# New tables of jobs, PSUM banks, engine order, adapter loads and diagonals in a fused adapter, state-space and mixture kernel

## Time and profile before

| | us |
|---|---|
| median of three runs (lowest, highest) | 960.28 (951.68, 961.02) |
| the profiled execution | 949.75 |
| its span, first to last instruction | 948.0 |
| PE (TensorE matmul) busy | 846.9 (89%) |
| DVE (VectorE) busy | 758.0 (80%) |
| POOL (GpSimd) busy | 659.5 (70%) |
| ACT (ScalarE) busy | 631.2 (67%) |

### The profile page before, as it was taken

How to read it: one execution, slowest core, us unless ns; L and a number is a source line. 1 busy time by engine, 2 the same in 40 slices (tenths; PEclk the granted TensorE clock), 3 DMA queues, 4 the chain that set the end, 5 groups by cost and what they waited for, 6 DMA issues and landing times.

```text
span 948.0 us, 18370 instructions
## 1 busy us (share of the span) xinstructions
PE 846.9 (89%) x6328; PEld 758.9 (80%) x6328; DVE 758.0 (80%) x677; ACT 631.2 (67%) x1467; POOL 659.5 (70%) x343
## 2 busy tenths in 40 slices
PE   5695898889997999889997999889997999788976
PEld 4573897789977998789987998789887998587773
DVE  3215776988989889988988889888988888999892
ACT  3227575867767776768767776668766776778650
POOL 1002676678877888668876887768877788889790
PEclk9897799999999999999999999999999999989896
DMA  9994687367662777376663777276773764243211
GB/s 252 316 310 137 222 251 211 107 198 243 171 213 87 274 205 217 109 237 213 170 218 105 255 205 235 78 250 201 194 212 113 223 170 148 90 145 84 90 62 44
DMA packets 165832, 172.23 MB, mean 182 GB/s; under 512 B 85225, under 2 KB 138473, under 8 KB 157550
## 3 DMA queue, kind: packets, MB, share of 16 engines
q1 hardware_dynamic: 143854, 94.12, 35.7%
q10 hardware_dynamic: 21888, 76.95, 23.5%
HBM read 137.33 MB, written 33.69 MB: 180 GB/s over the span
## 4 chain that ended last, share of the span: by engine, by line
PE 64%; DVE 15%; SPq 5%; POOL 5%; issue 4%; ACT 4%; DMA 2%; POOLq 0%; DVEq 0%; ACTq 0%
PE jb L956 28%; PE yp L1124 16%; DVE h L925 10%; PE dBx L956 9%; POOL hC L517 5%; PE yp L956 4%; PE jb L960 3%; PE yp L960 2%; SPq L316 2%; ACT dA L554 2%; SPq L391 2%; DVE Bd L757 1%; DVE dt L742 1%; PE yp L1129 1%; DVE xT L837 1%
## 5 line engine op out<-in xcount | busy, mean ns | idle before, releaser
L517 POOL TENSOR_TENSOR hC<-h,Cb 128x1024 f32<-128x1024 f32 x256 | 612.4, 2397 | 186.0 <-DVE h L925 178.2
L925 DVE TENSOR_TENSOR_SCAN h<-dA,dBx 128x1024 f32<-128x1024 f32 x256 | 583.1, 2281 | 62.6 <-PE dBx L956 51.1
L554 ACT ACTIVATE dA<-dt,negA 128x252 f32<-128x252 f32 x1024 | 430.2, 494 | 81.2 <-DVE h L925 69.8
L1124 PE MATMUL yp<-ident,hC 128*128 128x128 f32 x2048 | 279.7, 282 | 7.7 <-DVE HL L833 3.1
L956 PE MATMUL jb<-xT,Wst 128*128 128x256 f32 x1536 | 239.7, 300 | 17.3 <-DVE dt L742 8.5
L1124 PEld LDWEIGHTS yp<-ident,hC 128*128 128x128 f32 x2048 | 241.9, 146 | 10.7 <-POOL hC L517 7.9
L956 PEld LDWEIGHTS jb<-xT,Wst 128*128 128x128 f32 x1536 | 203.4, 196 | 22.9 <-DVE dt L742 9.9
L956 PE MATMUL dBx<-Bd,stacked 96*128 96x256 f32 x1024 | 189.8, 309 | 19.3 <-DVE h L925 10.0
L956 PEld LDWEIGHTS dBx<-Bd,stacked 96*128 96x128 f32 x1024 | 147.9, 198 | 44.2 <-issue 41.4
L502 POOL TENSOR_TENSOR dtx<-dt,u 128x256 f32<-128x256 f32 x64 | 47.4, 740 | 78.7 <-DVE dt L742 72.6
L579 ACT ACTIVATE HL<-yp 128x256 fp32r<-128x256 f32 x62 | 23.4, 377 | 42.1 <-PE yp L960 39.8
(11 more groups left out here) (145 smaller groups left out, 681.9 us busy)
## 6 DMA issues: line engine op xcount, KB each, us to landing
Wst<-W_scratch ACTq DMA_DIRECT2D x54, 1024.0 KB, 5.8
stacked<-dtx_scratch SPq DMA_DIRECT2D x192, 128.0 KB, 2.7
dtx_scratch<-HL SPq DMA_DIRECT2D x64, 256.0 KB, 2.5
Cb<-c_scratch SPq DMA_DIRECT2D x32, 512.0 KB, 5.5
W_scratch<-Wst ACTq DMA_DIRECT2D x8, 1024.0 KB, 6.1
xres<-in_x SPq DMA_DIRECT2D x64, 128.0 KB, 3.9
out<-obuf SPq DMA_DIRECT2D x32, 256.0 KB, 2.5
xin<-in_x ACTq DMA_DIRECT2D x28, 256.0 KB, 6.5
```

The source lines that it names most:

```text
L517: pool.tensor_tensor(hC[:, un % NHC, :].rearrange("p (n b t) -> p b n t", n=HS, b=2), h[:, un % NH, :].rearrange("p (b n t) -> p b n t", n ...
L554: act.activation(dA[:, half % NDA, :].rearrange("p (b n t) -> p b n t", b=GB_, n=HS)[:, :, n, 1:STEPS], dt[:, j % NDT, :].rearrange("p (b ...
L925: dve.tensor_tensor_scan(h[:, un % NH, :], dA[:, half % NDA, UNIT * p:UNIT * (p + 1)], dBx[un % 2][:, :], 0.0, ALU.mult, ALU.add).then_inc ...
L1124: last = pe.matmul(y, hC[:, un % NHC, P * n:P * (n + 1)], ident[:, :], is_transpose=True, start=un == 0 and n == 0, stop=False, skip_group ...
```

## The change

Only tables change: in which unit each job stands and in which order within one, the chunks of cond in each unit, some banks (xT 0 and 2, stack 7), which evacuations are late on ScalarE and VectorE, the units of `DTX`, `DU`, `ADAPTERS` and `DIAGONALS`, and a table of its own for group 0 in place of one derived from JOBS. The functions that read the tables stay, and so do the operations.

```diff
--- before.py
+++ after.py
@@ -38,50 +38,74 @@
 
 
 JOBS = {
-    (0, 0): [job("A2T", 0, "Y"), job("cond", 1, "A", (3, 5))],
-    (0, 1): [job("cond", 1, "A", (5, 8))],
-    (0, 2): [job("stack", 2, "Y"), job("x1T", 0, "B"), job("cond", 2, "A", (0, 6)), job("x1T", 1, "B")],
-    (0, 3): [job("cond", 2, "A", (6, 7)), job("x1T", 2, "B")],
-    (1, 0): [job("cond", 2, "A", (7, 8))],
-    (1, 1): [job("cond", 3, "A", (0, 3)), job("stack", 3, "Y"), job("x1T", 3, "B")],
-    (1, 2): [job("dtz", 2, "B"), job("cond", 3, "A", (3, 7))],
+    (0, 0): [job("cond", 1, "A", (1, 6))],
+    (0, 1): [job("cond", 1, "A", (6, 8)), job("A2T", 0, "Y")],
+    (0, 2): [job("stack", 2, "Y"), job("x1T", 0, "B"), job("cond", 2, "A", (0, 4)), job("x1T", 1, "B")],
+    (0, 3): [job("cond", 2, "A", (4, 6)), job("x1T", 2, "B")],
+    (1, 0): [job("cond", 2, "A", (6, 8))],
+    (1, 1): [job("cond", 3, "A", (0, 1)), job("stack", 3, "Y"), job("x1T", 3, "B")],
+    (1, 2): [job("dtz", 2, "B"), job("cond", 3, "A", (1, 7))],
     (1, 3): [job("cond", 3, "A", (7, 8))],
     (2, 0): [job("FB", 0, "Y"), job("mid", 0, "B", (0, 3)), job("cond", 4, "A", (0, 1))],
-    (2, 1): [job("cond", 4, "A", (1, 2)), job("stack", 4, "Y"), job("mid", 0, "B", (3, 6))],
-    (2, 2): [job("cond", 4, "A", (2, 5))],
-    (2, 3): [job("cond", 4, "A", (5, 6)), job("mid", 0, "B", (6, 8))],
-    (3, 0): [job("cond", 4, "A", (6, 7)), job("h2T", 0, "Y")],
-    (3, 1): [job("cond", 4, "A", (7, 8)), job("cond", 5, "A", (0, 3)), job("dtz", 3, "Y")],
-    (3, 2): [job("mid2", 0, "B"), job("cond", 5, "A", (3, 5)), job("rank", 0, None)],
-    (3, 3): [job("rank", 1, None), job("cond", 5, "A", (5, 8)), job("gate", 0, None), job("gate", 1, None)],
+    (2, 1): [job("cond", 4, "A", (1, 3))],
+    (2, 2): [job("stack", 4, "Y"), job("cond", 4, "A", (3, 4)), job("mid", 0, "B", (3, 6))],
+    (2, 3): [job("cond", 4, "A", (4, 5)), job("mid", 0, "B", (6, 8))],
+    (3, 0): [job("cond", 4, "A", (5, 6)), job("h2T", 0, "Y")],
+    (3, 1): [job("cond", 4, "A", (6, 8)), job("cond", 5, "A", (0, 1)), job("dtz", 3, "Y")],
+    (3, 2): [job("cond", 5, "A", (1, 3)), job("mid2", 0, "B"), job("rank", 0, None), job("rank", 1, None)],
+    (3, 3): [job("gate", 0, None), job("cond", 5, "A", (3, 8)), job("gate", 1, None)],
     (4, 0): [job("stack", 5, "Y"), job("cond", 6, "A", (0, 4))],
-    (4, 1): [job("gm", 0, "B"), job("cond", 6, "A", (4, 6)), job("out", 0, "B")],
-    (4, 2): [job("stack", 6, "Y"), job("cond", 6, "A", (6, 7)), job("out", 1, "B"), job("GAs", 0, None)],
+    (4, 1): [job("gm", 0, "B"), job("cond", 6, "A", (4, 5)), job("out", 0, "B")],
+    (4, 2): [job("GAs", 0, None), job("cond", 6, "A", (5, 7)), job("stack", 6, "Y"), job("out", 1, "B")],
     (4, 3): [job("cond", 6, "A", (7, 8)), job("cond", 7, "A", (0, 2))],
-    (5, 0): [job("cond", 7, "A", (2, 4))],
-    (5, 1): [job("cond", 7, "A", (4, 8)), job("out", 2, "Y"), job("xT", 0, "B")],
-    (5, 2): [job("stack", 7, "Y"), job("xproj", 0, "A", (0, 4)), job("xT", 1, "B")],
-    (5, 3): [job("xproj", 0, "A", (4, 8))],
-    (6, 0): [job("out", 3, "Y")],
-    (6, 1): [job("xT", 2, "A"), job("Bst", 0, "B"), job("xT", 3, "Y")],
-    (6, 2): [job("dtz", 4, "A")],
+    (5, 0): [job("cond", 7, "A", (2, 7))],
+    (5, 1): [job("cond", 7, "A", (7, 8)), job("out", 2, "Y"), job("xT", 0, "A")],
+    (5, 2): [job("stack", 7, "B"), job("xproj", 0, "A", (0, 4))],
+    (5, 3): [job("xT", 1, "B")],
+    (6, 0): [job("xproj", 0, "A", (4, 8)), job("out", 3, "Y")],
+    (6, 1): [job("xT", 2, "Y")],
+    (6, 2): [job("Bst", 0, "B"), job("xT", 3, "Y"), job("dtz", 4, "A")],
     (6, 3): [],
-    (7, 0): [job("cond", 0, "A", (0, 3), 2), job("xr", 0, "Y", (0, 4)), job("xr", 0, "Y", (4, 8)), job("stack", 8, "Y")],
-    (7, 1): [job("cond", 0, "A", (3, 7), 2), job("dtz", 5, "Y")],
-    (7, 2): [job("stack", 9, "Y"), job("cond", 0, "A", (7, 8), 2)],
-    (7, 3): [job("cond", 1, "A", (0, 3), 2)],
+    (7, 0): [job("xr", 0, "Y", (0, 4)), job("xr", 0, "Y", (4, 8)), job("cond", 0, "A", (0, 2), 2), job("stack", 8, "Y")],
+    (7, 1): [job("cond", 0, "A", (2, 4), 2), job("dtz", 5, "Y")],
+    (7, 2): [job("cond", 0, "A", (4, 8), 2), job("stack", 9, "Y")],
+    (7, 3): [job("cond", 1, "A", (0, 1), 2)],
 }
 
-FIRST = {at: [q for q in JOBS[at] if q[4] >= 0 and (q[0] != "cond" or q[4] == 2)] for at in JOBS}
-for _i in range(4):
-    FIRST[0, _i].append(job("xT", _i, "AB"[_i % 2], ahead=1))
-FIRST[0, 3].append(job("GAs", 0, None, ahead=1))
-FIRST[1, 0].append(job("xr", 0, "Y", None, 1))
-for _at, _q in (((2, 0), job("G2T", 0, "B", ahead=0)), ((2, 1), job("G2T", 1, "B", ahead=0)), ((2, 2), job("cF", 0, "B", ahead=0))):
-    FIRST[_at].append(_q)
-for _n in range(2 * K):
-    _q = FIRST[(5 + _n) // 4, (5 + _n) % 4]
-    _q.insert(min(1, len(_q)), job("cond", _n // 2, "A", ((0, 4), (4, 8))[_n % 2]))
+FIRST = {
+    (0, 0): [job("xT", 0, "Y", None, 1), job("xT", 1, "B", None, 1)],
+    (0, 1): [job("xT", 2, "A", None, 1)],
+    (0, 2): [job("stack", 2, "Y")],
+    (0, 3): [job("xT", 3, "B", None, 1), job("GAs", 0, None, None, 1)],
+    (1, 0): [job("xr", 0, "Y", None, 1)],
+    (1, 1): [job("cond", 0, "A", (0, 4))],
+    (1, 2): [job("dtz", 2, "B"), job("cond", 0, "A", (4, 8)), job("stack", 3, "Y")],
+    (1, 3): [job("cond", 1, "A", (0, 6))],
+    (2, 0): [job("cond", 1, "A", (6, 8)), job("G2T", 0, "B")],
+    (2, 1): [job("stack", 4, "Y"), job("G2T", 1, "B"), job("cond", 2, "A", (0, 3))],
+    (2, 2): [job("cF", 0, "B"), job("cond", 2, "A", (3, 8))],
+    (2, 3): [job("cond", 3, "A", (0, 4))],
+    (3, 0): [job("cond", 3, "A", (4, 8))],
+    (3, 1): [job("dtz", 3, "Y")],
+    (3, 2): [job("cond", 4, "A", (0, 4)), job("cond", 4, "A", (4, 8))],
+    (3, 3): [job("cond", 5, "A", (0, 4))],
+    (4, 0): [job("cond", 5, "A", (4, 8)), job("stack", 5, "Y")],
+    (4, 1): [job("cond", 6, "A", (0, 4))],
+    (4, 2): [job("stack", 6, "Y"), job("cond", 6, "A", (4, 8))],
+    (4, 3): [job("GAs", 0, None), job("cond", 7, "A", (0, 6))],
+    (5, 0): [job("cond", 7, "A", (6, 8))],
+    (5, 1): [job("xT", 0, "A"), job("stack", 7, "B")],
+    (5, 2): [],
+    (5, 3): [job("xproj", 0, "A", (0, 4)), job("xT", 1, "B")],
+    (6, 0): [job("xproj", 0, "A", (4, 8))],
+    (6, 1): [job("xT", 2, "Y")],
+    (6, 2): [job("Bst", 0, "B"), job("xT", 3, "Y"), job("dtz", 4, "A")],
+    (6, 3): [],
+    (7, 0): [job("xr", 0, "Y", (0, 4)), job("xr", 0, "Y", (4, 8)), job("cond", 0, "A", (0, 2), 2), job("stack", 8, "Y")],
+    (7, 1): [job("cond", 0, "A", (2, 4), 2), job("dtz", 5, "Y")],
+    (7, 2): [job("cond", 0, "A", (4, 8), 2), job("stack", 9, "Y")],
+    (7, 3): [job("cond", 1, "A", (0, 1), 2)],
+}
 
 SIXTH = {at: [q for q in JOBS[at] if q[4] < 2] for at in JOBS}
 FINAL = {at: [q for q in JOBS[at] if q[4] < 1 and not (q[0] == "dtz" and q[1] >= K // 2) and not (q[0] == "stack" and q[1] >= K)]
@@ -91,14 +115,14 @@
                 ((7, 1), job("mid", 0, "A", (2, 4), 0)), ((7, 2), job("mid", 0, "A", (4, 6), 0))):
     FINAL[_at].append(_q)
 
-LATE_ON_ACT = {"A2T", "Bst", "GAs", "cond", "dtz", "gate", "gm", "h2T", "mid2", "stack", "x1T", "xT", "xr"}
-LATE_ON_DVE = {"GAs", "cond", "dtz", "gate", "rank"}
-DTX = {(0, 0): 2, (0, 1): 3, (1, 3): 4, (2, 1): 5, (3, 3): 6, (4, 2): 7, (6, 2): 8, (7, 1): 9}
-DU = {(0, 1): 2, (1, 3): 3, (2, 2): 4, (3, 0): 5, (4, 1): 6, (5, 0): 7, (7, 0): 8, (7, 1): 9}
+LATE_ON_ACT = {"Bst", "FB", "GAs", "cond", "dtz", "h2T", "mid2", "out", "stack", "x1T", "xT", "xproj"}
+LATE_ON_DVE = {"A2T", "GAs", "dtz", "gate", "gm", "h2T", "rank"}
+DTX = {(0, 0): 2, (0, 1): 3, (1, 3): 4, (2, 1): 5, (3, 3): 6, (4, 2): 7, (6, 3): 8, (7, 0): 9}
+DU = {(0, 0): 2, (1, 3): 3, (2, 3): 4, (3, 1): 5, (3, 3): 6, (5, 0): 7, (6, 3): 8, (7, 1): 9}
 BANK_OF_B = next(q[2] for at in JOBS for q in JOBS[at] if q[0] == "Bst")
 LORA_A, LORA2, LORA_B = range(3)
-ADAPTERS = {(3, 3): 0, (4, 0): 1, (5, 3): 2}
-DIAGONALS = {(0, 0): 2, (0, 1): 3, (7, 0): 0, (7, 1): 1}
+ADAPTERS = {(3, 1): 0, (3, 3): 1, (5, 2): 2}
+DIAGONALS = {(0, 1): 3, (7, 0): 0, (7, 2): 1, (7, 3): 2}
 
 
 def layer_kernel(nc, x, ids1, ids2, W, loraA, loraB, A_log, Dw, xproj_w, dtproj_w, dtproj_b,
```

## The result

The changed kernel takes 963.5 us, the median of 18 runs (953.2 to 968.3); the kernel before took 955.5 on the same chips, also 18 runs (949.8 to 972.1). The ratio is 1.0056, interval 1.0029 to 1.0082. It leaves out executions more than 1.5% above the fastest of their kernel, and so is not the quotient of the medians (1.0084). I had forecast 953. The profiled execution is 963.8 us, span 962.0.

A forecast was written before the change was run, and what follows sets the result against it. TensorE's own work was taken to bound steady groups, with VectorE slower from (5,1) to (7,3). Gains of 8.4 - 1.5 + 0.6 = 7.5 us took the profiled 949.75 to 942.2, or 953 as median; range 937 to 969.

The forecast's parts named there:

- SP's queue: Adapter loads now directly ahead of stack 5's store; its loads might reach (5,0) late: 0.3 a group, five groups, 1.5 us lost.
- rival 1: Store 5 behind B2g lands 4.1 us late at (5,0) in groups 1 to 5: 20 us slower, 980; chance 0.19.
- Rows 7 and 8: Profile rows behind stack 5's store-to-landing times: 6.2 us in a steady group, 12.0 in group 0 directly behind B2g.
- this landing row: Stack 5's landing after the change, meant to tell whether a store waits for the small descriptors ahead on its ring.
- Pieces predicted: Steady group in three: (0,0) to (5,0) 61.9, to the scan of (7,1) 32.0, to the next (0,0) 8.95 us.
- the walk: Steady period followed stretch by stretch through the engines: 61.9 + 32.0 + 8.95 = 102.85 us, before 104.98.
- the middle of two counts: Steady period taken as 103.3 us, between 102.85 by stretches and 103.8 by work left plus waits: 1.7 won.
- The clock: Slow clock at group ends, a fall counted in half the groups: 1.7 - 0.85 + 0.55 = 1.4 us a group, 8.4 over six.
- the third wait: TensorE's new idle stretch of 1.5 us ahead of stack 9; a clock fall after it costs 1.7 us.
- my sign for it: If the forecast was right, the granted clock would be at 1.0 behind (7,2).
- the nothing I had: Last group, where VectorE's total counts and no operation is added or dropped: costed at 0, within 1 us.
- My +0.6: First group: same operations, stack 5's late landing stays; 0.6 us won, bounds -2 and +4.

The follow-up runs named there:

- adapters-only run: The kernel before with only the adapter loads moved to their new units (3,1), (3,3) and (5,2): 956.0 us, ratio 0.998.
- all three repairs: Changed kernel with cond 0's last chunk behind stack 9, adapter loads in their old units, C and residual loads ahead of stack 9: 952.8 us, ratio 0.9969.

## Why the prediction was wrong

**The step that failed is the term "SP's queue": "I take 0.3 a group for five groups, nearest to the steady row: 1.5 lost".** Its size was wrong, and a second loss of the same order stands at the group's end, where the sum had no transfer at all. Against the kernels without W's traffic, transfers cost the changed kernel 24.4 us (963.5 - 939.1) and the one before 11.7 (956.6 - 944.9): 12.7 lost where I had 1.5. Where it is lost can be read off VectorE's scans, block by block over groups 0 to 6, each trace less the one of the same tables without reloads. In the changed kernel W's traffic costs 9.2 us in blocks 0, 15.7 in blocks 4, 4.4 in blocks 5 and 2.9 in blocks 7, 31.0 in all; in the one before 3.6 in blocks 1, 5.0 in blocks 4 and 1.6 in blocks 5, 6.0 in all (that trace is a short one, three others of the old tables give 8.6 to 11.0; group 7, left out, is 5.9 us shorter in the changed kernel with the reloads than without, for a reason I did not look for). So about half of what is lost more lies in blocks 4 and 5, where the term stood, and half at the groups' ends, where nothing did.

The time of 963.5 lies inside my range of 937 to 969 and inside rival 1's "at half the price 962 to 970". The second fit is partly luck: rival 1 had the whole loss come from b(5,0). Point by point:

*The reload was not priced.* I put "cond 0's last four chunks" ahead of stack 9 and counted their columns on TensorE, but ScalarE's reload goes with them, 2.5 us nearer to store 8 and 2.6 us ahead of store 9, where it had been level. Cutting it gives 11.7 after the change and 3.8 before it. Sending it level with store 9 again gave back only 2.9 us by medians, so the lead alone isn't shown to be the reason.

*Did the cover go with the idle time?* That is my reading of the losses at the groups' ends. Before, store 9 also took 5.7 to 7.2 us at three ends, and b(1,0) waited for it in neither kernel; what came late stands behind its loads, C and the residual. The piece from the scan of (7,1) to (0,0) shrank from 11.29 to 8.93 us, and that would be the slack in which stack 8, stack 9, C and the residual came in. This is argued, not shown. Against it stands that taking C and the residual out of that line is worth the same by the ratios in both kernels (0.0018 and 0.0019), and that the residual leaves no later in the group than before; for it only the medians, 7.6 us after and 1.4 before.

*Rows 7 and 8 were misread.* I took group 0's 12.0 us from store 5 to landing as the price of a store right behind B2g. The changed kernel's steady group has that order, with one residual load between (HL is what the store sends; VectorE completes it):

```profile
366.40 4.81 SPq L340 DMA_DIRECT2D B2g<-in_L_cond_lora_B_w  x4
...
368.48 0.41 DVE L857 TENSOR_TENSOR HL<-yp,HL 128x256 fp32r<-128x256 f32 x1
...
371.26 0.59 SPq L361 DMA_DIRECT2D xres<-in_x  x1
371.97 0.40 SPq L384 DMA_DIRECT2D dtx_scratch<-HL  x1
374.67 1.29 SPq L391 DMA_DIRECT2D stacked<-dtx_scratch  x3
```

Once issued, the store lands in 2.7 us. In group 0 of the kernel before, what lies beside the loads of 154.03 is a reload:

```profile
153.98 0.35 ACTq L293 DMA_DIRECT2D Wst<-W_scratch  x1
154.03 1.29 SPq L367 DMA_DIRECT2D stacked<-dtx_scratch  x3
```

and in the changed kernel without reloads, where group 0's store 5 goes at 149.78 and its loads at 151.97, these take 2.2 and 2.5 to 2.7. So the 6 us landings of the earlier trace rows go with the reload on the other queue. The Trainium skill's rule of ring order (DMA: Bandwidth & Descriptors, section Queues, rings and completion order), which I had tied to this landing row, isn't borne out by it: behind B2g the store took 2.7 us.

The run of adapter loads did cost, but ahead of the store's issue, where I didn't look. HL was complete at 368.89 and the store left at 371.97, 3.1 us late. In groups 1 to 5 of the changed kernel this delay is 2.3 to 3.1 us and in group 0 6.4 (150.95 to 157.35, behind B2g, whose issue took 7.0 us, and a residual load of 4.1). Before the change it was 0.1 to 0.6, and 2.1 in group 0. It is 0.1 in all groups with the reloads cut, with the same order on SyncE, and 0.1 with the adapters spread: it takes both, the loads ahead on its own queue and W's traffic. With the adapters back it is 0.1 in group 0, but 2.1 to 2.8 in the others.

*Rival 1 happened, at about half its price.* W's traffic costs blocks 4 and 5 together 20.1 us in the changed kernel (13.7 and 20.8 in two other traces with the new adapter places), 10.1 to 16.3 in five traces of the new tables with the adapters back, and 6.5 to 8.0 in four of the old tables. A DMA is the releaser at b(5,0) in group 0 (4.2 us, 3.8 before) and in three of the five steady groups, by 1.2 to 2.3; in these the slowest of stack 5's loads also took 4.0 to 4.9 us, not 2.6. SyncE's run of loads grew: it issues adapters until 54.5 us behind the group's first scan (371.2 - 316.7), where before it was 50.1 (360.6 - 310.5), because stack 4 stands ahead of all of them. What the moved places are worth in whole runs, 3.1 us (alone back) to 4.6 (with the reload cut) by medians, is clear of noise in neither pair.

*The engines' side was right, and better than I took it.* Pieces predicted 61.9, 32.0, 8.95; measured 61.66, 32.27, 8.93. The wait for xT 3 is 1.97 (2.0 predicted), those ahead of stack 9 are 1.27 and 0.55 (1.5 and 0.55). That the sum comes out to the hundredth (102.85) is luck: two pieces are off by 0.2 to 0.3 in opposite directions. I should have kept the walk and not the middle of two counts. Without reloads the gain per steady group is 2.97 in groups 1 to 4 (105.83 to 102.86) and 2.4 in group 5, not 1.4, for there the kernel before has its slow clock ahead of xr in each of groups 1 to 4 (6 us at 0.57 in group 2), as I had supposed for every other one.

*The clock.* In the changed kernel the granted clock does fall behind the third wait, against my sign for it, in groups 2 to 5 of the six (I had counted half); in groups 0 and 1 it falls only earlier, behind the wait for xT 3. Here group 2, at the lower of the two levels (1.2 of 2.4 GHz):

```profile
418.30:421.00 2.70, 2.64 (x13) 2.67 (x14) 2.70 (x3) 1.20 (x4) 0.18 (x1) 0.50 0.80 286
```

It costs this group nothing there: from the scan of (7,1) to that of the next (0,0) are 11.15 us (410.68 to 421.83), and 11.08 without reloads, where it doesn't fall, since VectorE's chain sets that stretch; groups 4 and 5 have 11.09.

*The last groups and the tail.* Group 6 takes 102.1 against 100.1 before, for one quarter of the diagonals now stands in its last block (16.1 us against 14.4) and not in the first of group 7; that one takes 10.9 against 12.8. Together that is 0.2 us, near the nothing I had. The tail behind the last scan took 29.5 us against 26.4. The clock's timing differs there, the last additions and gates ran at 0.55 in this trace and 0.81 in the one of before,

```profile
936.00:948.00 12.00, 8.17 (x31) 6.35 (x31) 0.98 (x5) 0.97 (x2) 1.21 (x1) 0.55 0.00 0
```

```profile
924.00:935.00 11.00, 7.07 (x40) 5.58 (x40) 1.88 (x10) 1.18 (x3) 2.34 (x1) 0.81 0.00 0
```

and either tail occurs with either table (29.5 with the old one in the adapters-only run, 26.4 with the new one in the run with all three repairs), so I don't put it down to the tables.

*The first group.* My +0.6 was wrong in sign in this pair of traces: it is 3.5 us longer (121.0 against 117.4), its block 4 alone 4.5. Without reloads it is 0.4 shorter (110.5 against 110.9), so here too the engines' side held. Other traces scatter: 118.9 and 119.4 in two with the old tables, 117.0 with the new ones and C and the residual first.

*The base.* The profiled execution of before, 949.75, is below all 18 timed ones (949.8 to 972.1), and few of its transfers were late. I read the slack from it, and it may be larger there than in a median run, 956.

**Open.** The repaired kernel still waits 9.5 us for stacked operands and 6.6 for residuals. Where two transfers meet differs from group to group in every whole kernel, and I haven't found what sets it. Store 8 took 4.3 instead of 2.2 us at one handover before the reload was out (before the change 3.7 and 3.9 at two), and this isn't W's doing: with all reloads cut, stores 8 and 9 still took 3.4 to 4.6 us at several ends in both kernels, and I don't know beside what. That the lost slack, and not the new phase of the reloads, makes W's traffic dearer is not separated by any run. I didn't try the reload on SyncE's own queue, nor stack 4 back in (2,1).

## What to carry to other kernels

When a job moves, list the transfers that its end sets off on *any* queue and lay them beside everything in flight there: here W's reloads cost the old tables 11.7 us and the new ones 24.4, more than the new order won (5.9). Idle time of the bottleneck engine may be the cover of a transfer; before taking 2 us of it away, look for the loads that land inside it. Look not only at how long a transfer takes but at how long its issue was held behind others on its queue. When a repair fails, read its waits before naming the reason: the four-piece reload lost time on ScalarE and not on the transfers. And a run with the disputed traffic cut to a few bytes, on both kernels, separates in one step whether an order is worse or only its transfers are late.

## What the runs showed of the hardware

A store of 256 KB landed in 2.2 us at five of six handovers when it left ahead of the 1 MB reload of another engine (store 8, changed kernel) and in 5.3 to 6.8 us when it left up to 3 us behind it (store 9). When it left within 0.5 us of it, in the kernel before, it took 2.2 to 7.2, and with all reloads cut still up to 4.6.

Four loads of small pieces (B2g) held SyncE's queue for 3.7 us with W's reloads cut (at 142.06) and for 7.0 with them (at 146.07), both in group 0, and a store behind them left 6.4 us after its data was complete, against 0.1.

A 1 MB load took ScalarE's queue 0.33 us to issue as one DMA and 1.80 as four; 57.2 us of ScalarE's idle time and a kernel 1.4% slower (977.5 against 963.5) went with the four.

Idle times of TensorE of 1.27 and 0.55 us close together were followed by a granted clock of 0.50 in the changed kernel (418.3 to 421.0) and by 1.00 in the same place without reloads (400 to 404), where the clock had been at 0.74 on average from 387 to 392 us, behind the 1.97 us wait.
